# A graph kernel's first layer: ScalarE builds the one-hot for the edge sums, by a distance and a relu, in place of VectorE's comparison

## The reference

```python
h = (x @ W).reshape(n, HEADS, C)
a_src = jnp.einsum('nhc,hc->nh', h, att_src)
a_dst = jnp.einsum('nhc,hc->nh', h, att_dst)
e = a_src[src] + a_dst[dst]
e = jnp.where(e >= 0, e, NEG_SLOPE * e)
m = jax.ops.segment_max(e, dst, num_segments=n)
alpha = jnp.exp(e - m[dst])
denom = jax.ops.segment_sum(alpha, dst, num_segments=n)
alpha = alpha / (denom[dst] + 1e-16)
msg = alpha[:, :, None] * h[src]
out = jax.ops.segment_sum(msg, dst, num_segments=n)
```

## Time and profile before

| | us |
|---|---|
| median of 3 runs | 6718.57 |
| lowest and highest of the runs | 6707.67, 6720.85 |
| the profiled execution | 6709.51 |
| its span on the core | 6707.9 |
| the first layer's edges in it | about 135 to 1485 |

### The profile page before, as it was taken

One profiled execution on the slowest core, in us unless ns is written; L12 is line 12 of the kernel. 1 busy time (PEld: TensorE's weight loads), 2 busy tenths in 40 slices (PEclk: granted clock), 3 DMA queues, 4 the chain that ended last, 5 costly groups with the idle time before them and its releaser, 6 DMA issues. The chain is left out here.

```text
span 6707.9 us, 101753 instructions
## 1 busy us (share of the span) xinstructions
PE 4589.8 (68%) x18270; PEld 3405.7 (51%) x18271; DVE 4578.5 (68%) x11385; ACT 2738.4 (41%) x8093; POOL 4024.3 (60%) x3678
## 2 busy tenths in 40 slices
PE   5466666650566666787777777766577777777799
PEld 4234434430333333476666666655455555555688
DVE  4466666676454454587777777766489989888554
ACT  0233333335333333252111111113298899888543
POOL 2666666633666666426888888881377777777110
PEclk8666676675767777897777777778788898988899
DMA  7344444424555655426888888886466666666110
GB/s 239 104 107 107 111 108 109 107 78 159 171 176 176 183 177 177 123 67 119 136 135 136 136 135 137 135 116 225 147 182 190 182 187 187 187 183 180 37 32 28
DMA packets 698838, 940.86 MB, mean 140 GB/s; under 512 B 99488, under 2 KB 555552, under 8 KB 698721
## 3 DMA queue, kind: packets, MB, share of 16 engines
q0 software_dynamic: 270624, 580.57, 37.7%
q1 hardware_dynamic: 408658, 339.19, 17.8%
q10 hardware_dynamic: 19440, 19.79, 0.9%
HBM read 756.06 MB, written 183.11 MB: 140 GB/s over the span
## 5 line engine op out<-in xcount | busy, mean ns | idle before, releaser
L1864 POOL DMA_INDIRECT gcn<-c_update,c_target x784 | 1227.4, 1566 | 265.0 <-issue 203.8
L696 POOL DMA_INDIRECT e_rows<-hrow,e_idx x832 | 820.7, 986 | 465.0 <-issue 234.8
L2240 POOL DMA_INDIRECT s_rows<-kv,s_idx x832 | 800.4, 962 | 397.1 <-issue 214.3
L1249 POOL DMA_INDIRECT g_rows<-x,g_idx x784 | 772.5, 985 | 388.1 <-issue 228.6
L759 PE MATMUL psum<-e_rows,e_onehot 128*128 128x265 f32 x1664 | 667.1, 556 | 292.5 <-DVE acc L853 124.3
L1368 PE MATMUL psum<-g_rows,g_onehot 128*128 x1664 | 606.0, 527 | 217.5 <-ACT g_rows L1272 169.9
L2354 PE MATMUL psum<-queries_sums,s_spread 128*128 x1664 | 523.7, 469 | 261.8 <-issue 153.4
L1330 DVE TENSOR_TENSOR acc<-acc,psum 128x1024 f32 x208 | 253.7, 1220 | 592.2 <-DMA n_bias<-in_l_bias 338.8
L759 PEld LDWEIGHTS psum<-e_rows,e_onehot 128*128 128x128 f32 x1664 | 396.9, 264 | 501.5 <-DVE acc L853 217.5
L1368 PEld LDWEIGHTS psum<-g_rows,g_onehot 128*128 128x128 f32 x1664 | 418.8, 264 | 421.9 <-issue 346.8
L1841 ACT COPY acc<-psum 128x512 f32<-128x512 f32 x208 | 121.9, 586 | 1157.2 <-PE psum L1795 618.9
(11 more groups left out here) (381 smaller groups left out, 9433.8 us busy)
## 6 DMA issues: line engine op xcount, KB each, us to landing
g_attr<-in_edge_attr SPq DMA_DIRECT2D x196, 512.0 KB
acc<-rows_src SPq DMA_DIRECT2D x208, 256.0 KB
e_drow<-rows_dloc SPq DMA_DIRECT2D x208, 128.0 KB
acc<-in_edge_feat SPq DMA_DIRECT2D x832, 32.0 KB
s_drow<-rows_dloc SPq DMA_DIRECT2D x208, 128.0 KB
n_sums<-gcn SPq DMA_DIRECT2D x100, 256.0 KB
e_rows<-hrow,e_idx POOLq DMA_INDIRECT x832
edge_rows<-c_edge_rows SPq DMA_DIRECT2D x208, 64.0 KB
```

Source lines behind the costliest of these rows:

```text
L696: pool.indirect_dma_start(rows[u][:, s, 0:D + H], None, k.hrow, bass.IndirectOffsetOnAxis(ap=idx[u][:, s:s + 1], axis=0)).then_inc(gathere ...
L1249: pool.indirect_dma_start(rows[:, s, :], None, k.x1, bass.IndirectOffsetOnAxis(ap=idx[:, s:s + 1], axis=0)).then_inc(gathered[n % ROUND], 16)
L1864: pool.indirect_dma_start(k.gcn[a], bass.IndirectOffsetOnAxis(ap=target[:, at:at + 1], axis=0), update[:, at, :], None, compute_op=ALU.add ...
L2240: pool.indirect_dma_start(rows[at.u][:, st, 0:2 * D], None, k.kv, bass.IndirectOffsetOnAxis(ap=idx[at.u][:, st:st + 1], axis=0)).then_inc( ...
```

## The change

VectorE's `mark` goes. ScalarE gets one of its own: for each of the four steps it takes the distance |dloc - iota| (four activations of 128 columns, written as bf16 to the new tile `apart`), waits for them, and one activation of 512 columns makes relu(1 - distance), which is 1 at distance 0 and 0 at any other whole number. It stands in ScalarE's order behind the weighting of group q, for group q+1, and for the first group of a block behind the block's exponentials. The wait on `summed` (the sums of two groups before have left the buffer) moves along. VectorE writes a column of ones once, and ScalarE waits for the set-up once.

```diff
-    SETUP = 5
+    SETUP = 6
...
+        apart, one = sb("e0_apart", [P, GROUP, P], BF16), sb("e0_one", [P, 1])
+        apart_ready = sem("e0_apart_ready")
...
         @block.scalar
...
+            def mark(n, q):
+                g = n * GB + q
+                act.wait_ge(onehot_ready, g + 1)
+                for s in range(GROUP):
+                    ins = act.activation(apart[:, s, :], k.iota[:], ACT.Abs,
+                                         bias=k.dloc[:, bass.ds(g * GROUP + s, 1)], scale=-1.0)
+                ins.then_inc(apart_ready, 1)
+                act.wait_ge(apart_ready, g + 1)
+                act.wait_ge(summed, n * SB + (q - 1) * GROUP + 2 * SB)
+                act.activation(flat(onehot[q % 2][:]), flat(apart[:]), ACT.Relu, bias=one[:, 0:1], scale=-1.0
+                               ).then_inc(onehot_ready, 1)
+
+            act.wait_ge(cleared, SETUP)
...
                             weigh(n - 1, 1 - u, q)
+                            if q < GB - 1:
+                                mark(n - 1, q + 1)
...
                     act.activation(by_step(rows[u][:, :, D:D + H]), logit[:], ACT.Exp).then_inc(weight_ready, 1)
+                    mark(n, 0)
...
                 weigh(BLOCKS - 1, 1, q)
+                if q < GB - 1:
+                    mark(BLOCKS - 1, q + 1)
...
+            setup.tick(dve.memset(one[:], 1.0))
...
-            def mark(n, q):
-                wait_if_any(dve, summed, n * SB + (q - 1) * GROUP + 2 * SB)
-                one_hot(dve, k, onehot[q % 2], n * GB + q).then_inc(onehot_ready, 1)
...
-                            if q < GB - 1:
-                                mark(n - 1, q + 1)
-                        if q == GB - 1:
-                            mark(n, 0)
...
-                if q < GB - 1:
-                    mark(last, q + 1)
```

## The result

The changed kernel takes 6739.86 us (median of 8 runs, 6728.47 to 6754.18) against 6719.85 us for the kernel before on the same chip (8 runs, 6707.67 to 6731.85): ratio 1.0032, 95% interval 1.0022 to 1.0042. It is 20 us slower, where 69 us less were forecast. The profiled execution has a span of 6752.5 us and is a high one; at the last block head it is 23.5 us behind the profile before (1478.98 against 1455.5 us), and the rest of its distance lies in layers that the change doesn't touch, where two executions of one kernel also differ (its own eight runs lie up to 26 us apart).

What follows compares the result with a forecast made beforehand. VectorE's order was taken to set the 49.57 us block, half by work, half by slow issue. 1.2 + 1.8 = 3.0 us over 25 blocks is 75 us, less +4 and +2 in the last: net -69, 6645 us (8 in 10: 6570 to 6740).

Steps and rivals of the forecast that it cites:

- The price list: ScalarE's costs: four distances 1.26 us, one one-hot 1.93 us, a group's work from 1.91 to 3.84 us.
- 0.05 us: On ScalarE, estimated delay from the last distance's end being seen until the relu may start.
- The turn of the loop: Rival: a stall of 4.69 us at each of ScalarE's 12 turns, 56 us, leaving 13 us gain: 6701; chance 0.03.
- Three one-hots, all taken: Passes 5 to 7: VectorE's three one-hots leave the path, 3 x 0.60 = 1.8 us a block; bounds 1.2 and 1.8.
- 1.2 us of passes 0 to 4: Passes 0 to 4: VectorE's five one-hots fewer gain 1.2 us a block, between bounds of 0 and 3.0.
- 1.7 us a block, all before pass 4: ScalarE's weightings: slow issue, 34.6 us over 20 blocks; if it stays, group 4 is ready at 21.6 us.
- several us: TensorE may be this much later with group 4 unnoticed, as its sums came only at 31.9 us.
- ScalarE's own issue becomes slow: Rival, first ten us of a block: one-hots at 7.3 us, block about 4 us longer, +100 us, 6815; chance 0.18.
- the wait for the small exponential: ScalarE's 23.69 us wait for VectorE's L885; the prediction is wrong if it vanishes.
- ScalarE's pace in passes 0 to 4: Forecast at 3.84 us a group instead of 3.26; the prediction is wrong if it exceeds 4.5 us.
- VectorE's "issue" time grows by what the comparisons leave: Sign against the prediction: VectorE's idle issue time takes up the comparisons' room, at most 4.8 us a block.
- 41.3: GpSimd's gathers, 32 to a block, need about 41.3 us: a floor under the block's expected 46.6 us.

Runs made afterwards that it cites:

- after_moved: The changed kernel with 40 one-column memsets more in VectorE's set-up, on a slow chip: 6762.74 us, 1.0004 against the kernel before.
- after_again: The changed kernel once more, unaltered, on a slow chip: 6792.57 us, 1.0047 against the kernel before.
- before_loads: The kernel before, with VectorE loading the row number singly ahead of each sum of groups 0, 3 and 4; slow chip: 6814.8 us, 1.0060.
- after_loads: The changed kernel, with VectorE loading the row number singly ahead of each sum of groups 0, 3 and 4; slow chip: 6790.11 us, 1.0027.
- behind_pad40: The changed kernel with 40 set-up memsets more and each later one-hot behind its own group's weighting; slow chip: 6758.52 us, 1.0002 against the kernel before.
- before_pad80: The kernel before with 80 one-column memsets more in VectorE's set-up, on a quick chip: 6252.11 us, 1.0002 against the kernel before.
- none: The changed kernel with 40 set-up memsets more and no one-hots made in the loop (sums not the reference's): 0.9959 to 0.9974 on four quick chips.
- after_pad40: The changed kernel with 40 one-column memsets more in VectorE's set-up, on a quick chip: 6234.97 us, 0.9971 against the kernel before.
- both: The kernel before, with ScalarE also making the one-hots into buffers nobody reads; quick chips: 6252.6 us, 1.0001, and again 6251.12 us, 1.0006.

## Why the prediction was wrong

**The price list was right, but for one entry.** The distances took 387 ns (0.386 forecast), the relu 722 ns (0.71 forecast), a group on ScalarE 3.93 us on a quick chip (3.84). ScalarE's weightings ended 4.4, 8.3, 12.3 and 16.2 us after the head there, against 4.5, 8.4, 12.2 and 16.0 in the prediction. The entry is the "0.05 us" between the last distance and the relu: 0.12 us on the quick chip, but 0.9 us in the mean of a slow one (7.5 us for the eight of a block in after_moved).

**The turn of the loop was taken off the sum, and belonged in it.** It stood among the rivals at a chance of 0.03, on ScalarE and with 56 us. It came on VectorE, whose loop the change only shortened: 30 us (after_again against after_moved), 2.9 to 3.3 us a turn there and 2.3 to 3.4 in the first profile. The turns are ten, not the twelve of the prediction. The argument against it, that the longest idle time lies in the middle of a block, spoke of the loop as it lay before. The two programs as built show that the loop begins elsewhere; the prediction didn't ask what that does. By these 30 us alone the forecast would have been -39 us.

**"Three one-hots, all taken" (1.8 us) failed in passes 5 to 7.** From the last sum of group 4 to the next head (means of 22 blocks) the kernel before took 49.5 - 35.3 = 14.2 us and the changed one, on the same chip, 50.4 - 36.5 = 13.9; after_moved, on another chip, took 14.3. The pair on one chip with the loop well placed, before_loads and after_loads, took 13.1 and 12.2. Each mean is uncertain by 0.3 to 0.6 us, from block to block. So 0 to 1 us came of the 1.8. The one-hots are gone from the path, but VectorE's spreads and sums there wait longer: ahead of the spreads of pass 5 it was idle 1.7 us a block in after_moved instead of 0.6 before.

**"1.2 us of passes 0 to 4" failed too.** In after_moved the first sums of groups 0 to 3 start 8.6, 13.2, 16.4 and 20.7 us after the head, and before at 8.4, 12.8, 16.0 and 20.5. The last sum of group 4 starts at 35.8 and did at 35.3 (in the loads pair at 38.4 and 38.8). Between them lies the stretch with slow issue, and it moved: group 3's last sum starts at 28.9 instead of 23.5, and group 4's four are through 2.6 us after their first instead of 4.7. The two traces are from different chips, and the changed kernel alone took 50.4 us a block on one and 51.6 on the other; the large moves, of 5 us, are in the changed kernel's trace from the first chip as well (28.4 for group 3's last sum). The prediction had carried the slow issue of VectorE over as a fixed delay in a fixed place, and had put ScalarE's at 1.7 us a block, all before pass 4. On ScalarE it was 2.4 us in after_moved (53.4 us over 22 blocks), most of it 22 to 28 us after the head, in pass 4, where before ScalarE had no work that could be late; group 4's weights came at 23.2 and group 5's at 33.2 us, against 21.6 and 24. TensorE started group 4 at 28.6 us, where it had at 21.0; the prediction allowed for "several us" there without a cost, and behind_pad40 bears it out. So the rival "ScalarE's own issue becomes slow" was right about the kind, and a long way too high about the size.

**The signs against it.** Two of the three are there as they were named: the wait for the small exponential went from 23.69 us in one block, 436.9 us over the stretch, to 23.9 us in after_moved; and ScalarE's pace in passes 0 to 4 was 4.7 us a group (23.2 less 4.4, over 4). The third, that VectorE's "issue" time grows by what the comparisons leave, isn't: ahead of its sums "issue" fell from 127.4 to 77.6 us. All idle time there grew, from 255.3 to 316.4 us, and with half of the increments missing from the trace the name says little. On a quick chip the gathers need 40.3 us a block, not 41.3, a slip of no weight.

**What is shown and what isn't.** Shown: the loop's place costs 30 us on a slow chip and nothing on a quick one (before_pad80); ScalarE's work and its order are free on quick chips (none against after_pad40, both), where GpSimd's gathers bound the gain at 0.3 to 0.4%; the relu's wait isn't one for group 3's products, and an earlier start of group 4 on TensorE gains nothing on a slow one (after_moved, behind_pad40). Argued from traces: that the slow issue, and the waits that end late, take up the room. That part is some 60 us (69 forecast as gain, plus 20 measured as loss, less 30 for the loop's place), and its cause stays open. The kernels none and both would tell whether ScalarE's work has a share in it, and never ran on a slow chip. Open altogether: what makes a register instruction take 0.70 us, and a wait end microseconds late, on some chips, in some stretches of a block and on four engines. The recording of the trace is an untested rival here, as said above. The slowness doesn't go with the gathers, which GpSimd is busy with 62% of the time: 7.9% of VectorE's register instructions were slow during them and 7.0% outside of them.

The best version seen that computes the layer is after_moved, the same kernel as after_pad40: 0.9971 on a quick chip and 1.0004 on a slow one, against the changed kernel's 1.0047 there. behind_pad40 is level with it on the slow chip (1.0002) and had no run on a quick one.

## What to carry to other kernels

When an edit changes the number of instructions on an engine whose loop is long, ask where that loop lies before costing the edit: look at the instruction queue's packets and at the engine's idle time at its turns, and if they have grown, move the loop by some instructions of set-up and measure again. Before reading who waited for whom, count how many of the semaphore increments the trace has; here it had about half of them or fewer in time on the slow chips. Idle time called "issue" is no fixed price that stays where it is: work taken off such an engine can come back as idle time, and work given to a neighbour that idles through the same stretch may meet it too. And ask what the next floor is; here GpSimd's gathers left 0.3 to 0.4% to gain on a chip with quick issue.

## What the runs showed of the hardware that I had not expected

The place of a loop decides whether it stays held. Loops of VectorE, by the instructions ahead of them and their length, with the instruction packets over 390 to 1370 us (before_pad80: 300 to 1180 us, on a quick chip):

| kernel | ahead | length | packets |
|---|---|---|---|
| before | 342 | 439 | 1 |
| changed | 334 | 403 | 50 |
| after_moved | 374 | 403 | 1 |
| before_pad80 | 422 | 439 | 53 |
| before_loads | 355 | 485 | 0 |
| after_loads | 347 | 449 | 1 |

Where the borders lie no run shows, and two blocks of 256 would sort the same loops apart; it is the five packets a turn, and not six, that speak for 128. So this is argued, not shown. The Trainium skill, "Runtime: NRT & Kernel Launch", section "Instruction fetch mechanics", has blocks of 256 instructions (16 KiB), two of them, and a stall when a taken branch leaves them. The stall is seen here, at 2.3 to 3.5 us; the packets seen are of 8 KB, half of such a block.

The chips differ by 8% on the whole kernel (6250 against 6760 us), and the ratio of two kernels differs with them: the comparison's removal is worth 0.3% on one kind, and on the other nothing (after_moved) to 0.4% (the loads pair, 25 us, give or take 18).

Waits end late on the slow chips. TensorE's first product of group 4 starts 5.3 us after the last of its inputs is there (after_moved), against 0.3 us on a quick chip (after_pad40), and ScalarE's wait for its own distances ends up to 9.6 us late.
